# Planning the first expert slots from three blocks of nodes instead of four, and starting slot 0 between the last block's sums and its choice

## The chip, the cores and the metric

One core of a Trainium2 chip. The metric is the device time of the whole program in microseconds, here the median of three runs of the kernel before. A separate, profiled execution gives the trace.

## The reference, cut to what matters

3125 nodes with 128 features, 100,000 edges sorted by destination. A two-layer graph convolution with a layer norm comes first, then three layers with a mixture of experts, then an output projection and a layer norm. Each of the three expert layers does:

```python
agg = segment_sum(h[src], dst) / deg                        # 256 wide
logits = concatenate([h, agg]) @ router_W[l] + router_b[l]  # 8 experts
vals, idx = top_k(logits, 2); gates = softmax(vals)
weak   = relu(agg @ weak_W[l, e] + weak_b[l, e])            # 4 experts
strong = relu(agg @ strong_W1[l, e] + strong_b1[l, e]) @ strong_W2[l, e] + strong_b2[l, e]   # 4 experts
h = h + sigmoid(h @ conf_W[l] + conf_b[l]) * (the two chosen experts, weighted by the gates)
```

## The kernel before, in words

The program has five phases. A dense adjacency (3200 x 3200 in bf16, 25 pieces of 800 KB in HBM) is built first. Phases 0 and 1 are the two convolutions, phases 2, 3 and 4 the three expert layers. `p` is the phase, `b` one of NB = 5 blocks of 640 nodes (TB = 5 tiles of 128), `k` one of NK = 5 pieces of a block's adjacency. All five engines run hand-written lists of instructions; what one waits for is a semaphore count in the code.

**Sums.** In a phase TensorE goes through the blocks. Phase 2 (`gather`, L1507) multiplies bf16 pieces from a ring with three bf16 parts of the features; 25 matmuls per piece, tile t of the block into PSUM bank t. ScalarE evicts each bank (`evicted`, L1246), VectorE adds the parts up (`block_of_nodes`, L823, L824), TensorE turns the block's five tiles (L1478), ScalarE copies them (L1226, L1222), and TensorE multiplies by the input weights (L1487), all of this beside the next block's matmuls, at the places in `PLACES`. Phases 3 and 4 (`aggregate`, L1594) use f32 pieces, widened by ScalarE (L1326) into two buffers, and 512 columns per tile. There ScalarE takes the low sums (`low_sums`, L1341), VectorE adds the high ones (`aggregates`, L987) into `tmp`; `a_sumf` counts the tiles taken, and the next block's first five matmuls each wait for one. Beside the next block TensorE turns h and the sums in eight groups (`turn_group`, L1645, five tiles by 128 features in groups of three and two, copied by ScalarE at L1316) and forms 40 logit matmuls of nine columns (`tile_logits`, L1651).

**Choice.** VectorE takes the logits (`logits`, L997 and L998 in phase 2, L958 later), finds the two largest (`choose`, L963 to L981; L976 writes the choice that TensorE waits for), TensorE counts ranks (`ranks`, L1572, L1574), and VectorE turns them into places in the sorted array `xs_d` (`positions`, L932 to L945). GpSimd then scatters the block's rows to `xs_d` by ten indirect transfers (`scatter_tile`, L644).

**Slots.** After the blocks come SLOTS = 32 slots of M = 256 sorted rows of one expert. SyncE fetches a slot's rows (L540, three buffers `xsl`), VectorE copies the expert's first weights (`weights`, L1083, L1084), TensorE turns the rows (`slot_turn`, L1674, bank 4), ScalarE copies them (L1356), TensorE does the first layer (`slot_hidden`, L1685, banks 5 and 6, four parts), ScalarE the relu (L1359), TensorE the second layer (`slot_output`, L1696, banks 0 and 1), VectorE bias and gate (L1113, L1115), and GpSimd adds the rows to h in HBM by two indirect transfers (L669). TensorE's order is turn j+1, output j, first layer j+1.

**Which expert a slot belongs to** stands in tables that VectorE computes: `table_counts` (L1012 to L1026), `table_experts` (L1032 to L1039) and `table_places` (L1050 to L1070), 36 instructions, each waiting for the one before. They run twice. The early ones fill EARLY = 12 slots with full groups of 256 from the first four blocks; they stand behind the positions of block 3, in VectorE's list ahead of the last block's sums. The late ones (the other 20 slots) are spread over slots 2, 3 and 4. Every engine reads its table entries into registers four slots at a time (`loads`, LOAD = 4). The last block's scatters go in at slots 2 to 6, two transfers each.

**Around the end of a phase,** TensorE's order is: last aggregation; in phase 2 the block's turns and products (`turned_and_multiplied`), in phases 3 and 4 eight turn groups and 40 logits (`last_logits`); slot 0's turn and first layer; ranks of the last block; then the slots. VectorE's is: early tables, sums of the last block, slot 0's weights, (phase 2: products,) logits, choice, slots.

## Time and profile before

| | |
|---|---|
| median of 3 runs | 2031.82 us (2031.15 to 2037.95) |
| profiled execution | 2040.89 us |
| its span | 2039.1 us, 30707 instructions |
| TensorE matmul busy | 1772.0 us, 87% |
| TensorE weight load busy | 1376.1 us, 67% |
| VectorE busy | 892.9 us, 44% |
| ScalarE busy | 829.7 us, 41% |
| GpSimd busy | 619.0 us, 30% |
| mean granted TensorE clock | 0.907 of full speed |

The span goes from the first to the last instruction of the profiled execution. Each engine's busy time is a share of it, and a busy TensorE counts the same at 1.2 and at 2.4 GHz, so the granted clock (PEclk, 1.00 or 0.50 where it does not change within a row) is read beside it. A wait matters only where the engine that waits is the one the rest of the program waits for.

### The profile page before, as it was taken

Reading aid. Unit: us, or ns where it says so; the run is one execution under the profiler, and the core shown is the slowest. Engines: PE = TensorE matmul, PEld = TensorE weight load, DVE = VectorE, ACT = ScalarE, POOL = GpSimd, SP = SyncE. Lnnn points to the kernel's source line nnn. Section 1 sums busy time; section 2 is a strip of 40 time slices with the busy share of each in tenths; the row PEclk is TensorE's granted clock in tenths of the full one; section 3 lists DMA queues with packets and bytes.
Section 4 is the critical chain, followed back from the end, with each engine's and each line's share of the span. In section 5 each row is a group of like instructions: output and inputs, shape, how many; then the busy total and the mean of one; then the engine's idle time right before and its main releaser. Section 6 shows DMA issues by size and latency. Waiting matters only on the chain.

```text
span 2039.1 us, 30707 instructions
## 1 busy us (share of the span) xinstructions
PE 1772.0 (87%) x9747; PEld 1376.1 (67%) x9748; DVE 892.9 (44%) x2593; ACT 829.7 (41%) x1404; POOL 619.0 (30%) x593
## 2 busy tenths in 40 slices
PE   3856666589999998999979998999979998999974
PEld 2545555445566654888868877888868777888864
DVE  6589999834344335533321113433321113433324
ACT  6156666634322222333326563333336663333321
POOL 1044444300000033444430231544430221644430
PEclk9866666689999999999999998999989997999986
DMA  6970000034566783354448551454458541544441
GB/s 145 341 265 0 0 0 0 24 128 173 197 204 222 244 312 123 74 114 74 71 73 283 196 192 44 83 111 72 68 107 284 184 165 43 96 68 74 74 114 51
DMA packets 162537, 259.54 MB, mean 127 GB/s; under 512 B 27776, under 2 KB 136043, under 8 KB 162424
## 3 DMA queue, kind: packets, MB, share of 16 engines
q1 hardware_dynamic: 125960, 206.09, 31.5%
q0 software_dynamic: 36464, 51.98, 14.5%
q8 instruction: 67, 1.10, 0.2%
q14 instruction: 46, 0.38, 0.1%
HBM read 149.08 MB, written 108.94 MB: 127 GB/s over the span
## 4 chain that ended last, share of the span: by engine, by line
PE 76%; DVE 12%; issue 5%; ACT 3%; DMA 2%; DVEq 1%; SPq 1%; POOL 0%; ACTq 0%; POOLq 0%
PE psum L1685 17%; PE psum L1696 16%; PE psum L1507 14%; PE psum L1594 13%; DVE arena L764 7%; PE psum L1651 2%; PE psum L1487 2%; PE psum L1674 2%; PE psum L1422 2%; PE psum L1454 2%; PE psum L1452 1%; PE psum L1645 1%; PE psum L1718 1%; DVEq L764 1%; PE psum L1478 1%
## 5 line engine op out<-in xcount | busy, mean ns | idle before, releaser
L669 POOL DMA_INDIRECT h_rows<-arena,idx x192 | 312.9, 1629 | 420.5 <-DVE arena L1115 374.7
L1359 ACT ACTIVATE arena<-psum,b1c 128x256 f32<-128x256 f32 x384 | 181.8, 473 | 462.5 <-PE psum L1685 462.5
L1685 PE MATMUL psum<-arena 128*128 128x256 f32 x1536 | 360.6, 389 | 6.7 <-ACT arena L1356 6.7
L1696 PE MATMUL psum<-arena 128*128 x1536 | 347.4, 379 | 0.0
L1685 PEld LDWEIGHTS psum<-arena 128*128 128x128 f32 x1536 | 281.1, 193 | 70.9 <-ACT arena L1359 18.7
L1507 PE MATMUL psum<-arena 128*128 128x384 bf16 (+1 forms) x1875 | 316.9, 326 | 0.5 <-ACT arena L1243 0.2
L1696 PEld LDWEIGHTS psum<-arena 128*128 128x128 f32 x1536 | 284.6, 190 | 34.8
L764 DVE TENSOR_TENSOR arena<-arena 125x1200 bf16<-125x1200 bf16 (+1 forms) x300 | 282.4, 1008 | 20.4 <-PE psum L1454 19.5
L1507 PEld LDWEIGHTS psum<-arena 128*128 128x128 bf16 x1875 | 181.5, 98 | 125.7 <-ACT arena L1246 3.2
L644 POOL DMA_INDIRECT xs_d<-arena,pos x150 | 146.3, 976 | 390.4 <-DVEq L946 348.4
L1113 DVE TENSOR_TENSOR arena<-psum,arena 128x256 f32<-128x256 f32 x192 | 80.9, 421 | 378.2 <-PE psum L1696 377.0
L604 POOL TENSOR_TENSOR arena<-arena 128x100 bf16 x200 | 137.9, 689 | 253.3 <-ACT arena L1204 248.2
L1594 PE MATMUL psum<-halves,wide_a 128*128 128x512 f32 x650 | 171.3, 409 | 21.5 <-DVE halves L1120 20.4
L1206 ACT CAST arena<-psum 128x800 f32 x200 | 165.5, 828 | 0.2 <-issue 0.2
L1594 PE MATMUL psum<-halves,wide_b 128*128 128x512 f32 x600 | 153.8, 400 | 1.1 <-issue 1.1
L1594 PEld LDWEIGHTS psum<-halves,wide_a 128*128 128x128 f32 x650 | 121.8, 195 | 46.6 <-issue 23.4
L1454 PEld LDWEIGHTS psum<-arena 125*128 125x128 bf16 x1200 | 122.9, 134 | 25.0
L1454 PE MATMUL psum<-arena 125*128 125x100 bf16 x1200 | 139.6, 270 | 0.0
L1447 PE MATMUL psum<-arena 128*128 128x2 bf16 x200 | 37.5, 188 | 108.5 <-DVE arena L764 92.9
L1594 PEld LDWEIGHTS psum<-halves,wide_b 128*128 128x128 f32 x600 | 108.5, 188 | 22.1 <-issue 2.2
L1452 PE MATMUL psum<-arena 125*128 125x200 bf16 (+1 forms) x400 | 108.6, 369 | 0.0
L1447 PEld LDWEIGHTS psum<-arena 128*128 128x128 bf16 x200 | 21.8, 109 | 124.0 <-ACT arena L1206 61.1
(252 smaller groups left out, 1751.2 us busy)
## 6 DMA issues: line engine op xcount, KB each, us to landing
arena<-adj_d SPq DMA_DIRECT2D x54, 800.0 KB, 4.5
ring<-adj_d SPq DMA_DIRECT2D x46, 800.0 KB, 4.5
xs_d<-zrow SPq DMA_DIRECT2D x8, 3432.0 KB, 27.3
arena<-xs_d SPq DMA_DIRECT2D x96, 264.0 KB, 2.8
adj_d<-arena SPq DMA_DIRECT2D x25, 800.0 KB, 4.4
h_rows<-zrow SPq DMA_DIRECT2D x1, 8192.0 KB, 39.3
h_new<-h_rows SPq DMA_DIRECT2D x12, 640.0 KB, 8.0
arena<-h_rows SPq DMA_DIRECT2D x10, 640.0 KB, 6.7
```

The source lines that it names most:

```text
L604: pool.tensor_tensor(a, first_w[:, u % 8], a, ALU.add).then_inc(s_first, 1)
L644: pool.indirect_dma_start(xs_d, bass.IndirectOffsetOnAxis(ap=pos[:, b % 2, k, t:t + 1], axis=0), pay_of(p, b)[:, k, t], None).then_inc(a_s ...
L669: pool.indirect_dma_start(h_rows, bass.IndirectOffsetOnAxis(ap=idx[:, j % 2, h:h + 1], axis=0), ybuf[:, j % 2, h], None, compute_op=ALU.ad ...
L764: v.tensor_tensor(oh, every, keys.rearrange("p (n o z) -> p n o z", z=2, o=1).broadcast_to(shape), ALU.is_equal).then_inc(ready, 1)
L1206: act.copy(adj[:, bass.ds(off[u] + WC, G * WC)].rearrange("p (b n) -> p b n", b=2), banks[:, :, WC:WC + GA]).then_inc(s_wide, 1)
L1359: act.activation(hid[:, j % 2, f], psum[:, 5 + f % 2, 0:M], ACT.Relu, bias=b1c[:, bass.ds(at_b1[j % LOAD] + f, 1)]).then_inc(b_hidf, 1)
L1452: pe.matmul(bank[:, 0:cols], oh1[:, q, n, :, z % 2], ohe[:, q % 2, g, 0:cols, z], start=(z == 0), stop=False, skip_group_check=True)
L1454: mm = pe.matmul(bank[:, bass.ds(rel[(q % 2 * k + g) * (G - NST) + z - NST], WC)], oh1[:, q, n, :, z % 2], oh2[:, q, (g * (G - NST) + z - ...
L1507: return pe.matmul(psum[:, t, 0:width], ring[:, k, s, t * P:(t + 1) * P], features[p][:, k * SK + s, 0:width], start=(k == 0 and s == 0), ...
L1594: return pe.matmul(psum[:, t, :], adj32[(b * NK + k) % 2][:, s, t * P:(t + 1) * P], halves[:, k * SK + s].rearrange("p k f -> p (k f)"), s ...
L1685: mm = pe.matmul(psum[:, 5 + f % 2, 0:M], w1s[:, j % 2, f // 2, kt, f % 2 * P:(f % 2 + 1) * P], xsT[:, j % 2, kt], start=(kt == 0), stop=( ...
L1696: mm = pe.matmul(psum[:, h, 0:H], hid[:, j % 2, f, h * P:(h + 1) * P], w1f[:, bass.ds(at_w2 + f * H, H)], start=(f == 0), stop=(f == FT - 1))
```

## The change

EARLY goes from 12 to 7, and the early tables are computed after block 2's positions (three of five blocks) instead of block 3's. Slot 0's turn and first layer move ahead of the last block's turns and products (phase 2) or in between its turn groups (phases 3 and 4); they use banks 0, 1 and 2 for that, which the last block's first tiles leave first. VectorE copies slot 0's weights before it takes the last block's sums, and SyncE may fetch the first rows once the last block's third piece has been used (phase 2) or its last piece has been widened (3 and 4). Register groups follow EARLY: slots 0 to 3, 4 to 6, 7 to 10 and so on, the last of slot 31 alone. The late tables (25 slots) are computed at slots 1, 2 and 3, and the last block's scatters go in at slot 1 (two tiles, four transfers), 2 (two tiles) and 3 (one).

```diff
-EARLY = 12
+EARLY = 7
...
+        def turn_bank(j):
+            return 4 if j else 0
+        def hid_bank(j, f):
+            return (5 if j else 1) + f % 2
+        def group(j):
+            g = j - j % LOAD if j < EARLY else EARLY + (j - EARLY) // LOAD * LOAD
+            return g, min(g + LOAD, EARLY if j < EARLY else SLOTS)
...
 SyncE, slots_in
                 if p == 2:
-                    sp.wait_ge(s_agg, TB * 3 * NB)
+                    sp.wait_ge(s_piece, (3 * NB - 1) * (NK - 1) + 3)
                 else:
-                    sp.wait_ge(a_sum, sums_before(blk(p, NB)))
+                    sp.wait_ge(e_conv, piece_no(p, NB - 1, NK - 1) + 1)
                     if j == 0:
-                        rows_scattered(sp, blk(p, NB - 1))
+                        rows_scattered(sp, blk(p, NB - 2))
...
 GpSimd
-                    if j == 2:
+                    if j == 1:
                         rows_ready(p, NB - 1)
-                    if 2 <= j < 2 + TB:
-                        scatter_tile(p, NB - 1, j - 2)
+                    for t in {1: (0, 1), 2: (2, 3), 3: (4,)}.get(j, ()):
+                        scatter_tile(p, NB - 1, t)
...
 VectorE
+            def first_weights(p):
+                if p == 2:
+                    v.wait_ge(s_piece, (3 * NB - 1) * (NK - 1) + 2)
+                else:
+                    v.wait_ge(e_conv, piece_no(p, NB - 1, NK - 1) + 1)
+                v.wait_ge(s_wexp, 16 * NWD * (p - 1))
+                weights(p, 0)
...
-                    elif j == 2:
+                    elif j == 1:
                         table_counts(early=False)
-                    elif j == 3:
+                    elif j == 2:
                         table_experts(early=False)
-                    elif j == 4:
+                    elif j == 3:
                         table_places(p, early=False)
...
                 for b in range(NB):
+                    if b == NB - 1 and p == 2:
+                        first_weights(p)
...
-                    if b == (NB - 2 if p == 2 else NB - 1):
+                    if b == (NB - 3 if p == 2 else NB - 2):
                         table_counts(early=True)
                         table_experts(early=True)
                         table_places(p, early=True)
+                    if p > 2 and b == NB - 1:
+                        first_weights(p)
                     if p > 2:
                         aggregates(p, b)
...
 ScalarE, phases 3 and 4
+                    slot_biases(p, 0)
                     low_sums(p, NB - 1)
-                    turned(p, NB - 1)
+                    turned(p, NB - 1, (0,))
+                    slot_rows(p, 0)
+                    turned(p, NB - 1, (1,))
+                    slot_hidden(p, 0)
+                    turned(p, NB - 1, (2, 3))
...
 TensorE, last_logits
                 for n in range(8):
-                    if n == 4:
+                    if n == 2:
+                        pe.wait_ge(a_sumf, sums_before(i) + 1)
+                        slot_turn(p, 0)
+                        at_w2 = slot_places(p, 0)
+                    elif n == 4:
+                        pe.wait_ge(a_sumf, sums_before(i) + 3)
+                        slot_hidden(p, 0)
                         pe.wait_ge(a_sumf, sums_before(i + 1))
                     turn_group(p, NB - 1, n)
...
 TensorE, after the last block
                 if p == 2:
+                    pe.wait_ge(n_out, TB * (3 * NB - 1) + 1)
+                    slot_turn(p, 0)
+                    at_w2 = slot_places(p, 0)
+                    pe.wait_ge(n_out, TB * (3 * NB - 1) + 3)
+                    slot_hidden(p, 0)
                     pe.wait_ge(a_rankf, NB - 1)
                     for stage in range(3):
                         turned_and_multiplied(4 * NB - 1, stage)
                 else:
-                    last_logits(p)
-                slot_turn(p, 0)
-                slot_hidden(p, 0)
+                    at_w2 = last_logits(p)
                 ranks(p, NB - 1)
```

VectorE, phase 3, between block 2's positions and block 3's sums. In the rows `arena` is on-chip memory and the words behind "waits" are semaphores (`vector_steps_of_experts` is the link to the instruction before). Before:

```order
L943 CAST pos<-posf 128x10 [waits rows_scattered_1,rows_scattered_0,vector_steps_of_experts]
L944 COPY arena<-arena 128x10
L945 COPY arena<-goal 128x10
L987 SCALAR_TENSOR_TENSOR arena<-psum,rcol,arena 128x256 [waits vector_steps_of_experts,low_sums_taken]
L987 SCALAR_TENSOR_TENSOR arena<-psum,rcol,arena 128x256 [waits low_sums_taken] x4
L958 TENSOR_TENSOR arena<-psum,rbias 128x5x9 [waits logits_summed]
```

With the change, the positions' last row and the first of the table rows, then (33 rows further) the last two table rows and what follows:

```order
L960 COPY arena<-goal 128x10
L1027 TENSOR_TENSOR arena<-nxt,cap 128x8 [waits vector_steps_of_experts]
L1084 TENSOR_SCALAR arena<-arena 1x7 [waits vector_steps_of_experts]
L1085 TENSOR_SCALAR arena<-arena 1x7 [waits vector_steps_of_experts]
L1002 SCALAR_TENSOR_TENSOR arena<-psum,rcol,arena 128x256 [waits vector_steps_of_experts,low_sums_taken]
L1002 SCALAR_TENSOR_TENSOR arena<-psum,rcol,arena 128x256 [waits low_sums_taken] x4
L973 TENSOR_TENSOR arena<-psum,rbias 128x5x9 [waits logits_summed]
```

The 36 table rows now stand ahead of the sums of block 3 (L1002, L987 before), which TensorE's block 4 waits for.

VectorE, phase 3, between block 3's positions and the last block's logits, with the change (before, the 36 table rows stand where the two register loads, L413, stand below, and the loads and copies of the weights come after the sums):

```order
L959 COPY arena<-arena 128x10
L960 COPY arena<-goal 128x10
L413 TENSOR_LOAD arena [waits vector_steps_of_experts,expert_weights_in,expert_pieces_widened]
L413 TENSOR_LOAD arena
L1097 ISA
L1097 COPY arena<-arena 128x512
L1098 ISA
L1098 COPY arena<-arena 128x512
L1002 SCALAR_TENSOR_TENSOR arena<-psum,rcol,arena 128x256 [waits low_sums_taken] x5
L973 TENSOR_TENSOR arena<-psum,rbias 128x5x9 [waits logits_summed]
```

The weights' copies (L1097, L1098; L1083, L1084 before) have moved ahead of the sums, the tables have left.

TensorE, phase 3, from the last block's turn groups to the slots; of each group of rows the first is shown. Before:

```order
L1645 MATMUL psum<-ident,arena 128x128 [waits turned_taken,expert_aggregates_taken]
L1645 MATMUL psum<-ident,arena 128x128 [waits turned_taken]
L1651 MATMUL psum<-rw,arena 128x9 [waits logits_taken,turned_taken]
L1674 MATMUL psum<-ident,arena 128x128 [waits slot_turned_taken,slot_rows_in_2]
L1685 MATMUL psum<-arena 128x256 [waits slot_hidden_taken,slot_weights_ready,slot_turned_taken]
L1572 MATMUL psum<-sel,tri 128x48 [waits ranks_taken,choices_ready]
L1574 MATMUL psum<-sel,ones_s 128x40
L400 TENSOR_LOAD arena [waits slot_tables_ready]
```

With the change:

```order
L1693 MATMUL psum<-ident,arena 128x128 [waits turned_taken,expert_h_block_in]
L1693 MATMUL psum<-ident,arena 128x128 [waits turned_taken]
L1734 MATMUL psum<-ident,arena 128x128 [waits slot_turned_taken,slot_rows_in_2,expert_aggregates_taken]
L413 TENSOR_LOAD arena [waits slot_tables_ready]
L1693 MATMUL psum<-ident,arena 128x128 [waits turned_taken]
L1693 MATMUL psum<-ident,arena 128x128 [waits turned_taken]
L1745 MATMUL psum<-arena 128x256 [waits slot_weights_ready,slot_hidden_taken,slot_turned_taken,expert_aggregates_taken]
L1693 MATMUL psum<-ident,arena 128x128 [waits turned_taken,expert_aggregates_taken]
L1699 MATMUL psum<-rw,arena 128x9 [waits logits_taken,turned_taken]
L1620 MATMUL psum<-sel,tri 128x48 [waits ranks_taken,choices_ready]
L1734 MATMUL psum<-ident,arena 128x128 [waits slot_turned_taken,slot_rows_in_0]
```

Slot 0's turn (L1734, L1674 before), its register load (L413) and its first layer (L1745, L1685 before) have moved from behind the logits (L1699, L1651 before) to between the turn groups (L1693, L1645 before), so that nothing stands between logits and ranks.

## Rows read from the trace of the kernel before

**Rows 1.** Timeline, end of phase 2 (start us, us, engine, line, what, xcount [idle before <-releaser]).

```profile
800.08 0.58 ACT L1246 ACTIVATE arena<-psum,rcol 128x384 f32<-128x384 f32 x1 [0.24 <-PE psum L1507]
...
805.82 1.09 PE L1478 MATMUL psum<-ident,arena 128*128 128x128 f32 x4 [5.78 <-DVEq L835]
...
815.98 0.20 DVE L976 TENSOR_TENSOR sel<-arena 128x40 bf16<-128x40 f32 x1
...
817.00 6.23 PE L1685 MATMUL psum<-arena 128*128 128x256 f32 x16 [1.63 <-ACT arena L1356]
...
823.69 3.62 PE L1696 MATMUL psum<-arena 128*128 x16
```


**Rows 2.** Timeline, end of block 4 of phase 3: transposes, logits, choice.

```profile
1249.33 0.71 PE L1645 MATMUL psum<-ident,arena 128*128 128x128 f32 x5
...
1256.25 2.80 PE L1645 MATMUL psum<-ident,arena 128*128 128x128 f32 x10 [5.06 <-DVE arena L987]
...
1259.51 8.71 PE L1651 MATMUL psum<-rw,arena 128*128 128x9 f32 x40 [0.46 <-ACT arena L1316]
...
1270.70 0.20 DVE L976 TENSOR_TENSOR sel<-arena 128x40 bf16<-128x40 f32 x1
```


**Rows 3.** Windows: length, busy time (instructions) of PE, PEld, DVE, ACT, POOL, PEclk, DMA, GB/s.

```profile
815.00:816.00 1.00, 0.36 (x4) 0.12 (x2) 0.79 (x9) 0.21 (x1) 0.00 (x0) 0.65 0.74 226
...
1061.00:1062.00 1.00, 0.00 (x0) 0.00 (x0) 0.00 (x0) 0.00 (x0) 0.69 (x2) 0.53 0.00 0
...
1255.00:1256.00 1.00, 0.00 (x0) 0.00 (x0) 1.00 (x4) 0.00 (x0) 0.94 (x1) 0.80 0.37 135
1260.00:1268.00 8.00, 8.00 (x39) 8.00 (x40) 0.00 (x0) 2.42 (x2) 0.00 (x0) 0.50 0.34 103
```


**Rows 4.** The chain of waits, phase 3: start us, us, what.

```profile
1055.13 3.04 PE psum L1696 x14
...
1068.76 31.39 PE psum L1594 x125
...
1111.12 0.79 PE psum L1651 x8
...
1120.10 11.48 PE psum L1594 x50
...
1278.20 3.46 PE psum L1696 x16
```


**Rows 5.** Timeline, block 3 to block 4 of phase 3.

```profile
1208.14 0.17 DVE L945 COPY arena<-goal 128x10 f32<-128x10 f32 x1
...
1211.99 0.85 PE L1594 MATMUL psum<-halves,wide_a 128*128 128x512 f32 x3
...
1215.85 0.55 PE L1645 MATMUL psum<-ident,arena 128*128 128x128 f32 x3 [0.95 <-ACT arena L1316]
```


**Rows 6.** Timeline, first and last of the 36 table instructions, phase 3.

```profile
1245.51 0.17 DVE L1012 TENSOR_TENSOR arena<-nxt,cap 128x8 f32<-128x8 f32 x1
...
1253.77 0.22 DVE L1070 TENSOR_SCALAR arena<-arena 1x12 int32<-1x12 f32 x1
```


**Rows 7.** Timeline, block 3 to block 4 of phase 2.

```profile
770.98 0.18 DVE L945 COPY arena<-goal 128x10 f32<-128x10 f32 x1
...
776.67 0.83 DVE L823 TENSOR_TENSOR arena<-arena 128x640 f32<-128x640 f32 x1 [5.51 <-ACT arena L1246]
...
780.12 0.60 PE L1478 MATMUL psum<-ident,arena 128*128 128x128 f32 x4
```


**Rows 8.** Line L1674, all slots: TensorE's idle time before it (us, times).

```profile
  issue: 8.8, 21
```


**Rows 9.** Timeline, first copy of a slot's weights, and one of GpSimd's scatters.

```profile
808.24 0.43 DVE L1083 COPY arena<-arena 128x512 f32 x1 [2.62 <-issue]
...
839.97 0.99 POOL L644 DMA_INDIRECT xs_d<-arena,pos  x1 [0.30 <-issue]
```


**Rows 10.** The page, part 5: the adds of slot outputs (busy, mean ns, idle before).

```profile
L669 POOL DMA_INDIRECT h_rows<-arena,idx x192 | 312.9, 1629 | 420.5 <-DVE arena L1115 374.7
```

More of the change, by code:

```diff
@@ L1093, in slots @@
                     J = slot(p, j)
-                    if j % LOAD == 0:
+                    g = group(j)[0]
+                    if j == g:
                         at_b2 = loads(EDVE, 4, j, NS * H)
                     if j + 1 < SLOTS:
-                        weights(j + 1)
+                        weights(p, j + 1)
                     v.wait_ge(b_xin[J % 3], 16 * (J // 3 + 1))
@@ L1262, in rows, with slot_biases, slot_rows, slot_hidden @@
                 act.copy(pay[:, 1, :, 0:H], tmp).then_inc(a_pay, 1)
+            at_b1 = {}
+            def slot_biases(p, j):
+                if j == 0 or j == EARLY:
+                    act.wait_ge(b_tab, 2 * (p - 2) + (2 if j else 1))
+                at_b1[p, j] = loads(EACT, 5, j, (NL * NE - 1) * FT)
+            def slot_rows(p, j):
+                J = slot(p, j)
+                act.wait_ge(b_turn, J + 1)
+                act.copy(xsT[:, j % 2].rearrange("p f n -> p (f n)"), psum[:, turn_bank(j), 0:2 * M]).then_inc(b_xT, 1)
+            def slot_hidden(p, j):
+                J, g = slot(p, j), group(j)[0]
+                for f in range(FT):
+                    act.wait_ge(b_hid, 4 * J + f + 1)
+                    act.activation(hid[:, j % 2, f], psum[:, hid_bank(j, f), 0:M], ACT.Relu, bias=b1c[:, bass.ds(at_b1[p, g][j - g] + f, 1)]).then_inc(b_hidf, 1)
             def split_tiles(n, between):
@@ L1307, in _, with turned @@
                 act.wait_ge(n_turn, 2 * (n + 1))
+                if i == 3 * NB - 1:
+                    slot_biases(2, 0)
                 for t in range(TB):
                     evicted(i, t)
-            def turned(p, b):
+            def turned(p, b, some=range(4)):
                 i = blk(p, b)
-                for f in range(4):
+                for f in some:
                     for g, (t0, t1) in enumerate(GROUPS):
@@ L1349, in slots @@
                 for j in range(SLOTS):
-                    J = slot(p, j)
-                    if j == 0 or j == EARLY:
-                        act.wait_ge(b_tab, 2 * (p - 2) + (2 if j else 1))
-                    if j % LOAD == 0:
-                        at_b1 = loads(EACT, 5, j, (NL * NE - 1) * FT)
-                    act.wait_ge(b_turn, J + 1)
-                    act.copy(xsT[:, j % 2].rearrange("p f n -> p (f n)"), psum[:, 4, 0:2 * M]).then_inc(b_xT, 1)
-                    for f in range(FT):
-                        act.wait_ge(b_hid, 4 * J + f + 1)
-                        act.activation(hid[:, j % 2, f], psum[:, 5 + f % 2, 0:M], ACT.Relu, bias=b1c[:, bass.ds(at_b1[j % LOAD] + f, 1)]).then_inc(b_hidf, 1)
+                    if j:
+                        if j == group(j)[0]:
+                            slot_biases(p, j)
+                        slot_rows(p, j)
+                        slot_hidden(p, j)
                     if p < 4 and SLOTS - 2 * SK <= j < SLOTS - SK:
@@ L1665, in last_logits, with slot_places @@
                     tile_logits(p, NB - 1, t)
+                return at_w2
+            def slot_places(p, j):
+                if j == 0 or j == EARLY:
+                    pe.wait_ge(b_tab, 2 * (p - 2) + (2 if j else 1))
+                return loads(EPE, 3, j, 20 * 2 * M)
             def slot_turn(p, j):
@@ L1731, in _ @@
                 else:
[L1732 to L1734 removed]
+                    at_w2 = last_logits(p)
                 ranks(p, NB - 1)
                 for j in range(SLOTS):
[L1737 to L1740 removed]
+                    g = group(j)[0]
+                    if j and j == g:
+                        at_w2 = slot_places(p, j)
                     if j + 1 < SLOTS:
                         slot_turn(p, j + 1)
[L1743 removed]
+                    slot_output(p, j, at_w2[j - g])
                     if j + 1 < SLOTS:
```

49 lines of the change are left out of this document (24 added, 25 removed).

## The prediction

> **What bounds the kernel now.** I read the page first, for its busy times (in the table above): TensorE is the busiest by far, and no other engine comes near half the span. Then the timeline, at the places where the change sits: the end of each phase's last block, where five blocks of sums turn into 32 slots of expert work. There are three such passages (phases 2, 3, 4, at about 800, 1249 and 1704 us; the last two read alike). In phase 2 the last sum leaves PSUM at 800.66; TensorE does nothing for 5.8 us, turns and multiplies, and the first output product of slot 0 starts at 823.69 [rows 1]. In phase 3 the last block ends at 1249.3, TensorE waits 5.1 us for VectorE, works off the logits from 1259.51 to 1268.22, and slot 0's output starts at 1278.2 [rows 2, 4]. So a passage costs about 23.7 us in phase 2 and 28.9 us in phases 3 and 4. In them TensorE waits for VectorE or runs at 1.2 GHz; outside them it runs densely at 2.4.
>
> The clock has to be read with the durations. It falls some time after dense work stops: some 2.9 us after the last matmul at 1058.2, some 4.4 us after the transposes that end at 1251.2 (1256.25 less 5.06), and at about 815.3 in phase 2, soon after the products [rows 2, 3, 4] (a row of 1 us at 0.53, 0.80 or 0.65 was at the high level for 6, 60 or 30% of it). And 40 logits, TensorE busy all the time, do not bring it back: from 1260 to 1268 the granted clock is 0.50 [rows 3]. Starting low costs about 2.7 us: 125 matmuls take 31.39 us after a pause, where 50 take 11.48 in a dense stretch (28.7 for 125) [rows 4]. Logits cost 0.79 us per eight at the high clock, so 4.0 for 40, against 8.7 at the low one [rows 2, 4].
>
> **Part 1, the early tables one block sooner.** The tables are 36 small VectorE instructions, 8.5 us with their links [rows 6]. For 7 slots instead of 12, seven of them get shorter by some 0.04 us each; I take 8.2. What they no longer cover in the last block belongs to part 2. What they now hold up, one block earlier:
> - Phase 2: the choice of block 2 ends at 771.15, the tables would end at 779.4, and the sums of block 3, taken from 776.67 now, start 2.8 us later. TensorE wants them at 780.12 [rows 7]; they are done two operations of 0.86 us after 779.45, with signals at 781.3. A stall of 1.2 us.
> - Phases 3 and 4: positions end at 1208.3, so the tables end at 1216.6 and the first tile's sum at about 1217.2. TensorE's first matmul of block 4 overwrites that tile's bank and starts at 1211.99 now [rows 5]. It would wait 5.2 us, and the next four tiles come at 0.4 us each. Of the present schedule a wait of 0.95 us for ScalarE at 1215.85 goes: ScalarE is then free. The third group of transposes, at 1215.85 now, comes at about 1220.3: 4.5 us lost. Behind the waiting matmul stands all of block 4; nothing there has room to win it back (TensorE's own work follows without a gap).
> - The clock in that pause: nothing for 5.2 us, then single matmuls at 0.4 us for another 1.5. The first two falls above came 2.9 and 4.4 us after the last matmul, so I take it that it falls, and cost 2.4 us (bounds 0 and 2.7). Together 6.9 us in each of phases 3 and 4.
> Sum of part 1: 1.2 + 2 x 6.9 = 15.0 us lost (10.2 if the clock stays up).
>
> **Part 2, the passages.** Phase 2: the rows of slot 0 depend on blocks 0 to 2 alone, whose scatters end 15 us ahead; the weights are copied before 800 (two loads of registers and the copies, 3.4 us; now the idle time ahead of the copy is 2.62 us of that [rows 9]). TensorE turns slot 0 at 801.3 (1.2 us of part 1 in it), ScalarE copies when its evictions are over, and the first layer runs at full clock, 3.6 us instead of 6.23 [rows 1]. VectorE, without the tables, has the nodes ready 3 us sooner, so the turns wait for TensorE alone. Counted from the end of the aggregation: layer done at 5.1, products at 10.7 (an estimate from the 5.1 us that they take cold), choice 3.5 us later, ranks, slot 1's turn, output of slot 0 at 15.5, with 2.1 us for a clock that has fallen by then: 17.6, against 23.7. Gain 6.1.
>
> Phases 3 and 4, counted from the first transposes of the last block's h (1249.3 now): VectorE ends the positions at -4.0, copies the weights until -0.3 and has all five tiles by 1.9, not 6.8. TensorE: two groups, slot 0's turn, the register load, two groups, at 2.6 the first layer, over at 6.2; the four other groups, paced by ScalarE's copies of 0.4 to 0.5 us, until 8.6. Then 40 logits, at the high clock until it falls, some 4.5 us after the layer (10.7), so about 21 at 0.1 us and 19 at 0.218: done at 14.8 (bounds 12.6 warm, 17.3 cold). The choice is there 2.7 us later [rows 2], ranks and a slow turn bring slot 0's output to 18.9, and 1.8 us more is lost until the clock is back: 20.7 against 28.9. Gain 8.2 (bounds 5.5 and 12.5).
> Sum of part 2: 6.1 + 2 x 8.2 = 22.5 us gained.
>
> **Part 3, edits with one answer.** Slots now load in nine groups per phase, not eight. A group costs TensorE up to 0.42 us of idle [rows 8] (8.8 us, 21 times), lower bound nothing; 0.8 us for three, as the dense run hides part. The late tables move one slot ahead, with 25 slots: the places (19 of the 36 instructions, 4.5 us [rows 6]) now share slot 3 with register loads (up to 2.6 us [rows 9]), copies and the slot's own work, some 9.8 us in a slot of 7.4, but TensorE asks for that slot's result only 4 us after its output is done, and slot 4 has no table: nothing. The two adjacency pieces of 800 KB start at slot 7 instead of 12, with over 10 us before slot 7's rows are used: nothing.
>
> Sum: 15.0 - 22.5 + 0.8 = **-6.7 us**. Against the profiled execution (2040.89) that is 2034.2; I carry the difference to the median of the runs, 2031.82, and say 2025.1.
>
> **A rule of the skill.** The rows say that TensorE's clock fell in every pause above and did not rise during logits. The Trainium skill ("TensorE: Matmul & The Clock Gate", Part 1 and "Loop structure matters more than you think") says that the low clock is the default, that activity releases it, and that copies by another engine between groups of matmuls do not make TensorE cold, a long wait does. By it the filled passages would stay warm to the end, and the sum would be -11 to -20; that is the first rival. For the wait of part 1 page and rows agree.
>
> **The rivals.**
> 1. *The clock holds.* TensorE is hardly ever idle for more than 3 us in a passage, so it may stay at 2.4 GHz through logits and ranks: output at 16.4 in phases 3 and 4, a gain of 12.5 each; if the pause ahead of block 4 does not cool it either, only 4.5 is lost there. Total: 1.2 + 9.0 - 6.1 - 25.0 + 0.8 = -20, 2012 us; with one of the two alone about 2018. For it: TensorE has work in most of the passage. Against it: logits did not raise the clock [rows 3], and in phase 2 it fell at 815.3 with the products hardly over.
> 2. *The stall eats the gain.* The clock falls before the logits start: done at 17.3, gain 5.5 per phase, less than the 6.9 lost. Phase 2 alone wins, 4.9, perhaps less: 2 x 1.4 - 4.9 + 0.8 = -1.3, 2030.5 us. For it: the transposes from 6.2 to 8.6 are thin.
> 3. *Slower: GpSimd's scatters.* The last block's ten scatters go in at slots 1 to 3, four, four and two, where they were two per slot. One takes 1.3 us with its gap [rows 9], a slot's two adds 1.6 each and the same gaps, 3.8 [rows 10]: 9.0 us in a slot of 7.4. It is some 1.5 us late after slot 1, 3 after slot 2, and VectorE waits for slot 2's adds to land before it writes slot 4's indices. It costs nothing below a lateness of about 3.5 us plus VectorE's slack; if landings take longer under this load, each phase loses 8 us: -6.7 + 24 = +17, but part is caught up at slot 3; say 6 per phase and 2043 us. Against it: the sum stays just under that point.
> That seven full slots do not exist after three blocks is excluded: 3840 rows over eight experts leave at least 1800 in full groups of 256.
>
> **How the numbers follow.** Forecast 0.42, rival 1 0.28, rival 2 0.20, rival 3 0.10. The range takes in the warm case and all but the worst of rival 3: 2009 to 2039. A measurement here can tell 0.5% (10 us) from no change. Faster by more: rival 1 and the edge of the forecast, 0.30; slower by more: rival 3, 0.09; the rest 0.61.
>
> **What would show it.** In the changed profile: in block 4 of phases 3 and 4 the first aggregation matmul starts 5 us after block 3's last, with VectorE's table instructions before it (wrong if the pause is under 2 us), and the clock low in it. After the last block no wait of 5 us, slot 0's first layer at about 220 ns per pass; 40 logits in 4 to 8.7 us; slot 0's output about 15.5 us (phase 2) and 19 us (3 and 4) after the last aggregation. No TensorE idle time at slots 3 to 5 or 7; if there is, rival 3 holds.

## The result, and the profile after

The changed kernel takes 2019.95 us in the median (2018.26 to 2023.89, 6 runs) against 2034.88 (2031.15 to 2040.63, 6 runs) for the kernel before on the same chip: a ratio of 0.9929, 95% interval 0.9907 to 0.9952. Run again later (experiment e8) it took 2019.93 against 2033.90, 0.9937 (0.9916 to 0.9959). Forecast was 2025.1, within 2009 to 2039, as a gain of 6.7 us.

The stages that the change touches, from each trace. *Step* is the time from block 3's ranks to block 4's; *passage* from the end of the last aggregation to the start of slot 1's first layer (in brackets: to slot 0's first output product); *slots* from there to the end of slot 31. All in us, phases 2 / 3 / 4. Below, *behind the aggregation* is counted from the end of a phase's last aggregation, the clock is *low* where the granted clock is 0.50 (1.2 GHz), and a *record* is one matmul in the trace.

| kernel | step | passage | slots |
|---|---|---|---|
| before | 24.02 / 37.32 / 37.32 | 27.10 / 32.01 / 31.99 (23.64 / 28.55 / 28.53) | 231.44 / 231.13 / 231.15 |
| changed | 25.60 / 43.40 / 44.38 | 19.11 / 24.64 / 22.90 (14.09 / 18.80 / 17.40) | 231.46 / 231.33 / 231.32 |
| changed, again (e8) | 25.59 / 43.34 / 44.30 | 19.01 / 24.65 / 22.91 (14.42 / 18.92 / 17.47) | 231.49 / 231.45 / 231.36 |

So the steps lose 1.6 + 6.1 + 7.1 = 14.7, the passages win 8.0 + 7.4 + 9.1, 24.4 before rounding, the slots lose 0.4: **-9.3 us**; this sum is called the ledger below. In e8 the stages repeat within 0.1 us, passages to slot 0's output within 0.3. That is not so in every pair: the step of phase 4, the same program, is 44.38 here and 43.33 in e3, and e5 and e9, one program, have passages of 21.25 and 24.54 in phase 4. The whole does not: the first ranks of phase 2 come at 721.12 us before and at 712.80 in the changed kernel's profile, though both run the same program until then; e8 shows 709.35 and e9, whose program is also the same there, 721.09. A profiled span is therefore no measure of this change; its stages are.

The medians differ by about 5 us more than the ledger: the interval of the first comparison is -19 to -10, that of the second -17 to -8, so -9.3 lies just outside the one and inside the other. The ledger leaves out the stretches from the end of slot 31 to the next phase's first ranks (behind phase 4, to the end of the program). They took 72.8, 72.8 and 72.5 us before, 72.9, 71.5 and 69.7 in the changed kernel and 72.6, 71.4 and 69.3 in e8, 4.0 and 4.9 less in all. In the first 60 us of the last of them the mean granted clock is 0.63 before, 0.69 changed and 0.72 in e8. But e5 and e9, one program, differ there by 2.9 us (217.3 and 214.4 in all), and there is one trace of the kernel before; whether the change shortens these stretches is not shown.

**Phase 2**, timeline of TensorE in the changed kernel, against [rows 1, 7] (start us, us, engine, line, what, xcount, idle before and releaser):

```profile
773.58 0.63 PE L1526 MATMUL psum<-ident,arena 128*128 128x128 f32 x4 [1.38 <-DVEq L850]
...
793.37 0.60 PE L1734 MATMUL psum<-ident,arena 128*128 128x128 f32 x4
794.73 3.76 PE L1745 MATMUL psum<-arena 128*128 128x256 f32 x16 [0.76 <-ACT arena L1272]
...
802.62 0.69 PE L1535 MATMUL psum<-arena 128*128 128x266 f32 x2 [0.27 <-DVE arena L1013]
806.87 0.20 PE L1620 MATMUL psum<-sel,tri 128*128 128x48 bf16 x1 [3.57 <-DVE sel L991]
```

The first row is the stall of part 1, 1.38 where 1.2 was forecast. The wait of 5.78 and the cold layer of 6.23 of [rows 1] are gone: the turn runs at the end of the aggregation, the layer follows where the wait of 5.78 was and takes 3.76 at the full clock, products end at 803.31. The wait for the choice, 3.57, stays empty.

**Phase 3**, timeline, block 3 to block 4, VectorE and TensorE, against [rows 5, 6]; below it the windows (length, busy time and instructions of PE, PEld, DVE, ACT, POOL, granted clock, DMA share, GB/s):

```profile
1194.11 0.17 DVE L1027 TENSOR_TENSOR arena<-nxt,cap 128x8 f32<-128x8 f32 x1
...
1202.27 0.16 DVE L1085 TENSOR_SCALAR arena<-arena 1x7 int32<-1x7 f32 x1
1202.59 2.05 DVE L1002 SCALAR_TENSOR_TENSOR arena<-psum,rcol,arena 128x256 f32<-128x256 f32 x5 [0.16 <-DVE arena L1085]
...
1203.22 1.62 PE L1642 MATMUL psum<-halves,wide_a 128*128 128x512 f32 x3 [5.49 <-DVE arena L1002]
```

```profile
1199.00:1200.00 1.00, 0.00 (x0) 0.00 (x0) 0.86 (x5) 1.00 (x1) 0.69 (x2) 0.95 0.65 258
1200.00:1206.00 6.00, 2.78 (x8) 2.35 (x9) 4.10 (x17) 1.47 (x2) 4.65 (x5) 0.50 0.77 247
1206.00:1207.00 1.00, 1.00 (x5) 0.70 (x5) 0.00 (x0) 0.00 (x0) 0.82 (x1) 0.63 0.41 148
```

The tables take 8.3 us here; TensorE's matmul into the first tile's bank waits 5.49 for them (5.30 in phase 4), and the clock is low from 1199.9 to 1206.7. It fell 2.2 us after the last matmul; in phase 4 it fell 4.5 us after it and was low from 1653.9 to 1660.7, so there more of TensorE's work ran low.

**End of phase 3**, timeline of TensorE, against [rows 2], with the choice's last instruction and the windows, against [rows 3]:

```profile
1241.52 0.60 PE L1734 MATMUL psum<-ident,arena 128*128 128x128 f32 x4
...
1242.87 3.76 PE L1745 MATMUL psum<-arena 128*128 128x256 f32 x16
...
1247.67 0.77 PE L1693 MATMUL psum<-ident,arena 128*128 128x128 f32 x5 [0.48 <-ACT arena L1362]
1249.06 6.87 PE L1699 MATMUL psum<-rw,arena 128*128 128x9 f32 x40 [0.62 <-ACT arena L1362]
...
1258.60 0.20 DVE L991 TENSOR_TENSOR sel<-arena 128x40 bf16<-128x40 f32 x1
...
1259.94 6.00 PE L1758 MATMUL psum<-arena 128*128 x16
```

```profile
1249.00:1251.00 2.00, 1.94 (x18) 1.95 (x18) 0.00 (x0) 0.00 (x1) 0.96 (x1) 1.00 0.33 118
1251.00:1252.00 1.00, 1.00 (x8) 1.00 (x7) 0.00 (x0) 0.28 (x1) 0.00 (x0) 0.55 0.10 34
1252.00:1264.00 12.00, 9.07 (x39) 8.17 (x39) 5.18 (x39) 2.93 (x4) 0.00 (x0) 0.50 0.00 1
```

The wait of 5.06 of [rows 2] is gone. The last aggregation ended at 1241.14, the logits at 1255.93, 14.8 later; they took 6.87 (5.65 in phase 4) against 8.71, since the first ones ran before the clock fell, at 1251.1. Slot 0's output then runs low: 6.00 for 16 records, 3.46 before [rows 4].

### The profile page after: what moved, and what is told of

Its sections match the earlier page's. It is cut to its first block, busy times and chain, and to the rows that moved or that the text cites. A ratio compares the mean times of both kernels' runs of the same rounds, so it can differ in the third digit from the quotient of the medians.

```text
span 2017.7 us, 30733 instructions
## 1 busy us (share of the span) xinstructions
PE 1750.2 (87%) x9747; PEld 1363.5 (68%) x9748; DVE 894.8 (44%) x2593; ACT 828.5 (41%) x1404; POOL 614.5 (30%) x593
## 4 chain that ended last, share of the span: by engine, by line
PE 75%; DVE 12%; issue 5%; ACT 3%; DMA 2%; DVEq 1%; POOL 1%; SPq 1%; POOLq 0%; ACTq 0%
PE psum L1758 17%; PE psum L1745 17%; PE psum L1555 14%; PE psum L1642 13%; DVE arena L779 7%; PE psum L1734 2%; PE psum L1535 2%; PE psum L1699 2%; PE psum L1502 2%; PE psum L1470 1%; PE psum L1500 1%; PE psum L1693 1%; PE psum L1780 1%; DVEq L779 1%; ACT wide_a L1372 1%
## 5 line engine op out<-in xcount | busy, mean ns | idle before, releaser
L1745 PE MATMUL psum<-arena 128*128 128x256 f32 x1536 | 354.8, 384 | 1.0 <-ACT arena L1272 0.8
L1758 PE MATMUL psum<-arena 128*128 x1536 | 353.5, 384 | 0.0
L1745 PEld LDWEIGHTS psum<-arena 128*128 128x128 f32 x1536 | 276.4, 190 | 63.7 <-ACT arena L1306 20.4
```

The lines of the kernel that those rows point to most:

```text
L1745: mm = pe.matmul(psum[:, hid_bank(j, f), 0:M], w1s[:, j % 2, f // 2, kt, f % 2 * P:(f % 2 + 1) * P], xsT[:, j % 2, kt], start=(kt == 0), s ...
L1758: mm = pe.matmul(psum[:, h, 0:H], hid[:, j % 2, f, h * P:(h + 1) * P], w1f[:, bass.ds(at_w2 + f * H, H)], start=(f == 0), stop=(f == FT - 1))
```

## The experiments

Twelve runs were made, of ten new kernels: e8 is the changed kernel again, e9 is e5 again. The diffs show the lines that matter, not all. Every ratio is against the kernel before on the same chip, which took 2028 to 2044 us there in e1 to e10.

**e1, the tables behind the sums.** The early tables of phases 3 and 4 move from ahead of block 3's last sums to behind them; in phase 2 the counts and experts stay where they were and only the places go behind block 3's sums.

```diff
+                    if p > 2 and b == NB - 2:
+                        table_counts(early=True)
+                        table_experts(early=True)
+                        table_places(p, early=True)
```

> The changed kernel, with the early tables behind the sums that they held up: in phases 3 and 4 behind block 3's sums, in phase 2 the counts and experts before and the places after block 3's sums. Theory A (the tables ahead of block 3's sums cost 1.5 us in phase 2 and 6 to 7 us in phases 3 and 4, as the trace reads): TensorE's wait ahead of block 4 goes, and the time falls by 12 to 15 us against the changed kernel, to about 2006. Rival (the pause is only moved: the tables then hold up block 3's logits, or slot 0's rows come late): within 3 us of the changed kernel.

Measured: 2005.71 us (2004.90 to 2014.78), ratio 0.9876 (0.9831 to 0.9921). Steps 24.03 / 37.33 / 37.33, passages 19.11 / 24.72 / 22.92. TensorE's first matmuls of block 4 of phase 3 have no wait before them:

```profile
1193.21 0.85 PE L1647 MATMUL psum<-halves,wide_a 128*128 128x512 f32 x3
```

The 14.7 us of part 1 are an order, not a price: the same instructions, behind what TensorE waits for, cost nothing.

**e2, slot 0's turn and first layer where they were.** The tables stay early, TensorE and ScalarE get the order and banks of before.

```diff
-                    at_w2 = last_logits(p)
+                    last_logits(p)
+                slot_turn(p, 0)
+                slot_hidden(p, 0)
                 ranks(p, NB - 1)
```

> The changed kernel, with slot 0's turn and first layer back behind the logits (products in phase 2) on TensorE and ScalarE, in their old banks; VectorE, SyncE and GpSimd as changed. Theory A (the passage got shorter because slot 0's work fills it, as the prediction costed it): 3 to 6 us slower per passage, 2030 to 2038. Rival B (it got shorter because VectorE no longer computes tables there; slot 0's first layer filled the wait for the choice before and leaves it empty now): within 4 us of the changed kernel, with slot 0's output at full clock and the first layer at half.

Measured: 2027.84 us (2023.01 to 2031.23), ratio 0.9977 (0.9959 to 0.9995). Passages 24.22 / 25.25 / 23.59. So of the 24.4 us of the passages, 18.0 come from what e2 keeps of the change, above all VectorE without its tables (before to e2: 2.9 + 6.8 + 8.4), and 6.4 from slot 0's move (e2 to changed: 5.1 + 0.6 + 0.7). Each of the two theories is right in its part: A in phase 2, B in phases 3 and 4. There the move brings slot 0's output about 3 us forward (21.79 to 18.80 in phase 3) and gives most of it back in the output:

```profile
1258.43 6.42 PE L1728 MATMUL psum<-arena 128*128 128x256 f32 x16 [2.53 <-ACT arena L1300]
...
1265.31 3.62 PE L1739 MATMUL psum<-arena 128*128 x16
```

This is e2's timeline at the end of phase 3. The layer behind the choice runs low, but by the output the clock is up again (0.23 us a record, 0.38 in the changed kernel). With the layer gone from there, the output is the work that runs low.

**e3, the layer in the wait for the choice.** Slot 0's turn stays early, its layer goes behind the logits (phase 2: the products); e4 has e1's edit too.

```diff
                     at_w2 = last_logits(p)
+                slot_hidden(p, 0)
                 ranks(p, NB - 1)
```

> The changed kernel with slot 0's turn where the change puts it, its first layer behind the logits (products in phase 2), so that it fills the wait for the choice, and the exponents between its relus. If rival B holds: TensorE's 2.9 to 3.6 us of wait ahead of the ranks go and slot 0's output runs at full clock; 3 to 4 us per passage, about 2010. If the first layer between the sums and the logits is the better place: 2020 or more.

Measured: 2017.00 us (2014.82 to 2024.71), ratio 0.9920 (0.9898 to 0.9942). Passages 18.20 / 22.11 / 22.11: 4.2 us less in all than the changed kernel's; the two ratios can't be told apart. The expectation was too good. The order does pay by the stages, and the output runs at the full clock as it said, but the layer runs wholly low (6.31 us), which is longer than the wait for the choice, and the ranks now wait for the layer (phase 3).

**e4, both.**

> The first and the third of these together. Independent savings add up: about 1997 (1994 to 2003). If one eats the other (a clock that stays up without the pause makes the wait for the choice shorter anyway): 2003 to 2008.

Measured: 1999.35 us (1994.75 to 2006.75), ratio 0.9842 (0.9799 to 0.9885): faster than both kernels. The stages of its own trace account for it: 14.7 of the steps and 7.9 of the passages (16.19 / 20.50 / 22.08) from 2019.95 gives 1997.3. Of the 7.9, 3.7 are more than e3 has, though the edits to the passage are e3's. They go with the clock: in phase 2 it was low from 2.5 to 9.3 us behind the aggregation in e3 and never in e4, in phase 3 it fell at 6.5 and at 8.2. Part of that can be chance, since e10, whose program is e4's in phase 2, was low there from 3.7 to 7.2 and has 17.28. TensorE at the end of its phase 3:

```profile
1228.43 0.77 PE L1699 MATMUL psum<-ident,arena 128*128 128x128 f32 x5 [0.35 <-ACT arena L1367]
1229.82 5.49 PE L1705 MATMUL psum<-rw,arena 128*128 128x9 f32 x40 [0.62 <-ACT arena L1367]
1235.17 6.20 PE L1749 MATMUL psum<-arena 128*128 128x256 f32 x16
1241.21 0.19 PE L1626 MATMUL psum<-sel,tri 128*128 128x48 bf16 x1
```

**e5, TensorE busy in the pause**: 72 matmuls whose result nothing reads, ahead of block 4's aggregation. **e8 / e9** are the changed kernel and this one again, on one chip.

```diff
+                if b == NB - 1:
+                    fill(72, 5, 0)
```

> The changed kernel with 72 bf16 matmuls (ones by ones, 128x128, into columns of bank 5 that nothing reads) issued by TensorE ahead of block 4's aggregation in every phase that has one, so behind block 3's last products and in the pause of 5.3 to 5.5 us; nothing is left out of the computation. The step from block 3's ranks to block 4's was 43.40 and 44.38 us in phases 3 and 4, where without a pause it is 37.32. The pause itself explains 5.49 and 5.30, so 0.6 and 1.8 us are left for the clock of 0.50 that follows it. Theory A (the rest is the clock, and any matmuls hold it): the 72 matmuls end before VectorE's conversion, the clock stays at 1.00, the steps become 42.8 each, time about 2.2 us under the changed kernel's, 2017.7. Theory B (the clock doesn't go by whether the queue is busy but by how wide the work is): it falls all the same, the 72 take twice as long and end behind the conversion, steps of 45 to 47 us, time 2022 to 2025.

e5: 2019.73 us (2015.09 to 2024.39), ratio 0.9935 (0.9908 to 0.9961), so no difference to the changed kernel in the medians; but its steps were 42.04 and 41.76. Hence the pair:

> The changed kernel itself once more, beside the next one on the same chip, since the two profiled executions differ by 5.3 us ahead of the first rank of phase 2, where they are the same program. Both theories expect 2019.95 give or take 2 us, and steps of 43.4 and 44.4 us from block 3's ranks to block 4's in phases 3 and 4.

> The changed kernel with the 72 matmuls in the pause, in more runs. In one profiled execution they held the clock at 1.00 through the pause (steps of 42.04 and 41.76 us) and the passages behind were 1.6 us shorter each, 7.0 us in all, but the median of its runs equalled the changed kernel's. Theory A (the 7 us are real and were covered by what varies ahead of phase 2): 4 to 7 us under the changed kernel on the same chip. Theory B (the time comes back elsewhere, or the profiled execution was an odd one): within 1.5 us of it, and steps in its profile that are not the same as before.

e8: 2019.93 us (2015.28 to 2027.35). e9: 2015.19 us (2012.92 to 2023.86), ratio 0.9901 (0.9886 to 0.9917). Timeline and window of e9 at the pause of phase 3:

```profile
1205.40 4.19 PE L1640 MATMUL psum<-ones_s 128*128 128x128 bf16 x72
1211.06 1.19 PE L1646 MATMUL psum<-halves,wide_a 128*128 128x512 f32 x3 [1.46 <-DVE arena L1002]
```

```profile
1205.00:1210.00 5.00, 4.60 (x75) 4.16 (x73) 4.25 (x23) 3.22 (x2) 3.84 (x4) 1.00 0.70 261
```

The clock stays at 1.00 and the steps are 42.05 and 41.86, against 43.34 and 44.30 in e8. So the low clock behind the pause costs 1.3 us in phase 3 and 2.4 in phase 4, and the pause itself 4.6. What it costs goes with when it falls: 4.5 us after the last matmul in phase 4 of the changed kernel, but 2.4 in e3, whose step there is 43.33 without any added matmul. e9's passages, 23.02 and 24.54, sum to e8's (24.65, 22.91); e5's, 23.01 and 21.25, were 3.3 less in all, which didn't repeat: in phase 4 the clock fell 12.0 us behind the aggregation in e5 and 9.9 in e9. Of theory A's 7 us the steps' 3.7 are real and the passages' are not; the medians differ by 4.7.

**e6 and e10, half of the last logits earlier.** e4 with half of the last block's logits (kt 0 and 1 of the four parts, kt, that each logit sums) between and right behind the last turn groups.

```diff
+                        part_logits(p, range(TB), 0)
+                    elif n == 6:
+                        pe.wait_ge(a_turnf, turns_before(i) + 4)
+                        part_logits(p, range(2), 1)
                     turn_group(p, NB - 1, n)
+                part_logits(p, range(2, TB), 1)
```

> The fourth version (tables behind the sums, slot 0's first layer in the wait for the choice) with the last block's logits in phases 3 and 4 taken apart: kt 0 of all tiles ahead of turn group 4, kt 1 of two tiles ahead of group 6, of three behind group 7, and only kt 2 and 3 (20 of the 40 records) behind the last copy. Nothing is left out of the computation. The fourth version shows TensorE waiting 0.47, 0.35 and 0.62 us for ScalarE between these groups and 5.49 us of logits behind them in phase 3, 7.49 in phase 4. Theory A (the chain to the choice is TensorE's, and the early half fits in these waits): 1.2 to 1.5 us less in each of the two passages, 2.7 in all, time 1996.6 if the fourth version repeats its 1999.35. Theory B (the clock, which falls about 3.5 us into narrow matmuls, falls as much sooner): the first layer and the slot's output then run longer at 0.50, and no more than 1 us is gained in all: 1998.5. Theory C: the logits' early half delays ScalarE's copies of the last turns by more than it fills: 1 to 2 us slower.

> The sixth experiment with the start flag on the first of the early logits alone instead of on the first of each tile: there each tile's opening matmul made the next one into the tiles ahead of it overwrite instead of add, so that kt 0 of tiles 0 to 3 was missing from the last block's logits in phases 3 and 4. The same instructions in the same order, so both theories expect the same times: passages of 21.4 and 21.7 us, 1999 us, and the fall of the clock about 7 us behind the last aggregation though TensorE is then never idle. If its time differs by over 2 us, the sixth's passages depended on the data, and theory A of the sixth (1996.6) is open again.

In e6 the sums of the last block's logits in phases 3 and 4 lack kt 0 of tiles 0 to 3, as the text of e10 says; e10 has them whole. e6: 1999.07 us (1998.50 to 2001.67), ratio 0.9831 (0.9801 to 0.9861). e10: 1997.22 us (1991.99 to 2006.06), ratio 0.9817 (0.9788 to 0.9845). Neither can be told from e4. The logits did end sooner (10.1 us behind the last aggregation of phase 3 in e4, 8.0 in e6, 7.5 in e10), but the ranks came later there, at 17.0 instead of 16.0; in phase 4 they came at 17.0 instead of 17.6. Passages of phases 3 and 4 are 21.43 / 21.66 in e6, 21.70 / 21.70 in e10. Timelines of e10, TensorE, ScalarE and GpSimd:

```profile
1234.84 3.19 PE L1711 MATMUL psum<-rw,arena 128*128 128x9 f32 x26
1237.88 2.94 PE L1763 MATMUL psum<-arena 128*128 128x256 f32 x8
1243.96 3.78 PE L1763 MATMUL psum<-arena 128*128 128x256 f32 x8 [3.14 <-ACT arena L1311]
```

```profile
1241.12 1.26 ACT L1292 COPY arena<-arena 128x1280 f32<-128x1280 f32 x1 [5.54 <-issue]
1242.28 1.26 ACT L1293 COPY arena<-arena 128x1280 f32<-128x1280 f32 x1
1243.44 0.83 ACT L1311 ACTIVATE arena<-psum,b1c 128x256 f32<-128x256 f32 x2
```

```profile
1227.28 0.96 POOL L659 DMA_INDIRECT xs_d<-arena,pos  x1 [24.99 <-DVEq L961]
...
1238.62 0.96 POOL L659 DMA_INDIRECT xs_d<-arena,pos  x1 [0.30 <-issue]
```

The layer has two banks for its four results, so its second half waits for the relus. These stand behind ScalarE's two payload copies, and the copies, by the code, for the buffer that GpSimd's ten scatters of block 3 read, one per 1.26 us, the last from 1238.62. The copies start 10.6 us behind the last aggregation in the changed kernel, in e4 and in e10 alike. In e4 TensorE comes to its second half only when they are over, and shows no wait. In e10 this chain takes the place of the logits; the three theories had only the clock and the copies of the turns. That the relus wait for the copies is in the rows; that the copies wait for GpSimd is read from the code and the times (the profile names no releaser), and no experiment here shows it.

**e7, matmuls with 128 columns among the logits** of e4.

```diff
                 for t in range(TB):
+                    fill(6)
                     tile_logits(p, NB - 1, t)
```

> The fourth version with six bf16 matmuls (ones by ones, 128x128, into columns of bank 7 that nothing reads) ahead of the last block's logits of each of the five tiles, in phases 3 and 4: 30 in a phase. Nothing is left out of the computation. In the fourth version the clock fell 3.6 us into the logits of phase 3 and 1.4 us into those of phase 4, and the logits, the first layer (6.20 us for 16 records, 3.72 at full clock) and the start of slot 0's output ran at 0.50. Theory A (TensorE's narrow logits are what lets the clock fall, and work with 128 columns among them holds it): the 30 cost 0.055 each, 1.7 us; logits take 4 instead of 5.5 and 7.5, the layer 3.7 instead of 6.2, so passages shorter by 1.5 to 4 us each after the cost; time 1994 to 1997. Theory B (the waits for ScalarE between the last turn groups, 1.4 us in all, are what lets it fall): it falls at the same moment, and the 30 cost 1.7 to 3.3 us in each phase: 2003 to 2006.

Measured: 2009.18 us (2006.18 to 2013.90), ratio 0.9885 (0.9854 to 0.9917); passages 16.19 / 23.62 / 25.21, 6.3 us longer than e4's in all, and the time is past theory B's 2003 to 2006 too. Windows of e7 and, below, of e6 at the end of phase 3:

```profile
1235.00:1238.00 3.00, 3.00 (x36) 3.00 (x36) 0.00 (x0) 0.00 (x0) 2.21 (x3) 1.00 0.30 104
1238.00:1248.00 10.00, 10.00 (x42) 8.90 (x40) 2.97 (x26) 3.49 (x6) 0.66 (x1) 0.50 0.07 25
```

```profile
1231.00:1238.00 7.00, 6.95 (x60) 6.48 (x59) 1.49 (x4) 3.77 (x10) 5.37 (x6) 1.00 0.31 110
1238.00:1239.00 1.00, 1.00 (x7) 1.00 (x7) 0.00 (x0) 0.00 (x0) 0.80 (x1) 0.53 0.37 135
```

In e7 the clock falls at 1238.0, 8.4 us behind the last aggregation, as in e4 (8.2), and in phase 4 at 6.0 in both: the added matmuls hold nothing and cost their time. That refutes theory A. But theory B, that the waits for ScalarE let it fall, does not stand either: in e6 these waits are filled, TensorE is busy 6.95 of the 7 us from 1231, and the clock falls all the same, 6.7 us behind the aggregation (8.0 in phase 4; 8.2 and 8.1 in e10). What holds it in such a stretch stays open.

**e11 and e12, the relus ahead of the payload copies**, on e10 and on e4.

```diff
-                    rows(p, NB - 1)
-                    slot_hidden(p, 0, (0, 1))
-                    exponents(p, NB - 1)
-                    slot_hidden(p, 0, (2, 3))
+                    slot_hidden(p, 0)
+                    rows(p, NB - 1)
+                    exponents(p, NB - 1)
```

> The tenth experiment with one change of order on ScalarE in phases 3 and 4: slot 0's four relus ahead of the two payload copies of the last block (1.26 us each) and its exponents, instead of behind the copies and around the exponents. Nothing is left out of the computation. In the tenth the copies start 10.5 us behind the last aggregation, when GpSimd starts the last of block 3's ten scatters, which go at 1.26 us each, and end at 13.0; TensorE, with two banks for the layer, waited 3.14 us in the middle of it for the relus and gave the ranks 16.96 us behind the aggregation, though the choice was ready at 10.5. Theory A (GpSimd's scatters, by way of the copies, hold the relus and so the layer and the ranks): logits over at 7.3, the layer without a wait until about 13 (the clock falls at its start), ranks at 13.3 to 13.8, passages 18.2 instead of 21.7 in both phases, 1990 to 1991 us against 1997.2. Theory B (the layer would have ended late anyway, since TensorE is at the low clock): ranks at 15.5 or later, 1995 or more.

> The fourth version (logits whole, behind the last copy) with the same change of ScalarE's order as in the eleventh: relus, then payload copies, then exponents. Nothing is left out of the computation. In the fourth, the logits end 10.0 us behind the last aggregation of phase 3, the copies run at 10.6 to 13.0, and TensorE's layer at the low clock takes 6.2 us without a wait. Theory A (there TensorE is what binds, the copies are over before the relus matter): no change, 1999 give or take 2, passages of 20.5 and 22.1 give or take 0.5. Theory B (the relus bind there too): 2 us or more less in each passage, 1995.

Measured on a chip where the kernel before itself takes 2110.20 us: e11 2083.06 (2075.84 to 2093.19), ratio 0.9882 (0.9819 to 0.9945); e12 2088.51 (2070.50 to 2092.26), ratio 0.9880 (0.9806 to 0.9953). Both traces show the clock at 0.50 for up to 24 us at a time in the blocks of phases 3 and 4 (a step between ranks is up to 50.7 us where all others show 37.3), so their passages (e11 28.24 and 27.56, e12 28.03 and 28.19 in phases 3 and 4) compare with no other run. e11's TensorE timeline:

```profile
1288.23 4.43 PE L1710 MATMUL psum<-rw,arena 128*128 128x9 f32 x20 [1.45 <-ACT arena L1367]
1292.52 6.35 PE L1762 MATMUL psum<-arena 128*128 128x256 f32 x16
```

The wait in the middle of the layer is gone, but that proves nothing: the layer starts here 16.0 us behind the aggregation, past the 13.0 at which the copies of e10 were over. By its ratio neither kernel is faster than the one it was made from (e10 0.9817, e4 0.9842), and e11's 1990 us would have been 0.979 on e10's chip, outside e11's interval. Neither pair of theories is decided, and the order of the relus stays untested at the other chips' clock.

## Why the prediction was right

The result lies in its range, and by the stages its forecast, not a rival, is what happened; the gain was larger than the 6.7 us forecast, 9.3 by the stages and 14 to 15 by the medians. The time alone would not say so: 2019.95 lies nearer to rival 1 with one of its halves (2018) than to 2025.1. The traces decide, and in them the clock is low in the pause and in the passages.

- **Part 1**: 15.0 forecast, 14.7 measured. Phase 2: 1.2, measured 1.6. Phases 3 and 4: 6.9 each, measured 6.1 and 7.1, made up as forecast: 4.5 for the wait (4.6), 2.4 for the clock (1.3 and 2.4, by e8 and e9). The clock fell 2.2 us after the last matmul in phase 3 and 4.5 in phase 4, against 2.9 to 4.4 in the prediction. Its 2.9 takes the end of the work, 1058.2, from the chain; TensorE's own timeline has it at 1058.6, so 2.4:

```profile
1054.97 3.62 PE L1696 MATMUL psum<-arena 128*128 x16
```

- **Part 2**: 22.5 forecast, 24.4 measured, and here one term was mis-sized. Phases 3 and 4, 8.2 each: measured 7.4 and 9.1, with logits done at 14.8 (forecast 14.8) and 13.6, slot 0's output at 18.8 (18.9) and 17.4. That 14.8 met 14.8 is in part luck: the logits began at 7.9, not 8.6, and took 6.9 us, not 6.2, as the clock fell at 10.0, not 10.7. Phase 2, 6.1: measured 8.0. The estimate of the products from cold ones was too high (done at 9.8, forecast 10.7), and the output came at 14.1, not 15.5.
- What the text did not see is **which half of the change pays** in phases 3 and 4. It costed the passage as one piece; e2 shows 15.2 of the 16.5 us there without slot 0's move, and 0.6 and 0.7 from it, because the low clock then meets the output instead of the layer. It named that loss (1.8 us until the clock is back), but never asked what the passage would be without the move.
- **Part 3**: 0.8 forecast, 0.4 measured. The idle time before slot turns (L1734, all slots) is no higher than in [rows 8]:

```profile
  issue: 8.2, 20
```

- **Rival 1** (the clock holds) is refuted: it fell in the pause and in the passages. The rule that stood for it, in the Trainium skill ("TensorE: Matmul & The Clock Gate", "Loop structure matters more than you think"), is that copies by another engine between groups don't break TensorE's warmth. The prediction took from it that filled passages stay warm, and they didn't: no wait in the last 8 us before the fall at 1251.1 was longer than 0.62 us. Of the copies themselves the trace says nothing against the rule, since in e6 the clock fell with their waits filled. **Rival 2** (the clock falls ahead of the logits) did not come: it fell 2.0 us into them (3.4 in phase 4). **Rival 3** (GpSimd's scatters at slots 1 to 3) is refuted by the slots, 231.33 and 231.32 against 231.13 and 231.15. GpSimd's scatters of the block before do seem to bind, by the reading of e10, but only once the rest is out of the way.
- The excess of the medians over the stages, some 5 us, has no step in the prediction. In the traces the stretches behind the slots are 4.0 and 4.9 us shorter, which may be it; the cause is open.

## What to carry to other kernels

Before a block of small instructions is moved to an earlier turn, ask what it stands ahead of there: here the same tables cost 14.7 us ahead of the sums that TensorE wants and nothing behind them. When two edits touch one passage, cost each without the other, since the one that empties the passage may leave little for the second. And where runs vary by more than the effect, compare stages that repeat, not spans.

## What the runs showed that I had not expected

- Behind a dense stretch, TensorE's clock fell though it was kept busy, by turns, logits and their weight loads: 6.7 us (e6), 8.2 (e4) and 8.4 us (e7, with 30 more matmuls) behind the last aggregation of phase 3, and 10.0 in the changed kernel, where slot 0's layer lies between. In phase 4 it was 8.0, 6.0, 6.0 and 11.3, and much of the difference between passages of one program goes with this moment. In the pause, 72 matmuls of 0.058 us held it.
- The program ahead of phase 2 takes between 708.65 and 721.12 us in twelve profiled executions (all but e11 and e12), though its instructions are the same.
- One chip gave the kernel before 2110 us, 3.8% more than the others, with the clock at 0.50 for long stretches inside the blocks of phases 3 and 4 (in e11 and e12), and TensorE's waits of up to 4.7 us for which the profile names no releaser.
